# C rows spread by transposes of a broadcast column instead of one bf16 matmul, and unit 7 of each step turned like the other odd units

## The reference, cut to what matters

```python
xs = jnp.concatenate([x_hwwh, x_hwwh[..., ::-1]], axis=1)          # 4 paths, L = 128
x_dbl = jnp.einsum('bkdl,kcd->bkcl', xs, x_proj_w)                 # 8 + 16 + 16 rows
dts, Bs, Cs = jnp.split(x_dbl, [DT_RANK, DT_RANK + D_STATE], axis=2)
dts = softplus(einsum('bkrl,kdr->bkdl', dts, dt_projs_w) + dt_projs_b)
def step(h, inp):                                                  # for each of the 128 positions
    u, dt, Bl, Cl = inp
    h = h * jnp.exp(dt[..., None] * A) + (dt * u)[..., None] * Bl[:, :, None, :]
    return (h, jnp.einsum('bkdn,bkn->bkd', h, Cl))                 # D_STATE = 16 states n
```

## Time and profile before

| | |
|---|---|
| median of three runs | 29268.55 us |
| the profiled execution's own time | 29284.73 us |
| its span, first to last instruction | 29282.9 us |
| PE busy | 23746.5 us (81%) |
| DVE busy | 25685.0 us (88%) |
| ACT busy | 23805.4 us (81%) |
| POOL busy | 23349.3 us (80%) |
| mean granted TensorE clock | 0.946 |

### The profile page before, as it was taken

One profiled execution on the slowest core, in us unless ns is written; L12 is line 12 of the kernel. 1 busy time (PEld: TensorE's weight loads), 2 busy tenths in 40 slices (PEclk: granted clock), 3 DMA queues, 4 the chain that ended last, 5 costly groups with the idle time before them and its releaser, 6 DMA issues.

```text
span 29282.9 us, 495306 instructions
## 1 busy us (share of the span) xinstructions
PE 23746.5 (81%) x145198; PEld 17788.1 (61%) x145198; DVE 25685.0 (88%) x24511; ACT 23805.4 (81%) x48778; POOL 23349.3 (80%) x10372
## 2 busy tenths in 40 slices
PE   5999995888888888887888888888878888888887
PEld 1656563666666666666666666666666666666666
DVE  7555555999999999999999999999999999999999
ACT  2444444998889899888888888898888888998888
POOL 4000003999999999999999999999999999999999
PEclk6999997999999999999999999999999999999999
DMA  4000003333333333333333333333333333333333
GB/s 143 26 27 26 26 27 139 108 106 106 107 106 108 106 107 106 106 107 107 106 106 106 105 108 106 107 106 106 107 107 106 107 106 107 106 106 108 106 108 97
DMA packets 2189273, 2869.65 MB, mean 98 GB/s; under 512 B 695002, under 2 KB 964858, under 8 KB 2177786
## 3 DMA queue, kind: packets, MB, share of 16 engines
q1 hardware_dynamic: 2181978, 2803.33, 31.2%
q10 hardware_dynamic: 4608, 33.82, 0.3%
HBM read 2667.01 MB, written 169.74 MB: 97 GB/s over the span
## 4 chain that ended last, share of the span: by engine, by line
ACT 27%; PE 25%; issue 16%; DVE 11%; POOL 3%; ACTq 1%; DVEq 1%; DMA 0%; SPq 0%; POOLq 0%
DVE hst L1535 10%; PE yps L1245 8%; ACT dbT L1425 6%; ACT dAs L1403 6%; ACT dA L1403 6%; PE dbx L1230 5%; PE misc L1145 5%; PE misc L1164 2%; POOL hc L1612 2%; POOL dbu L1598 1%; DVE hc L1543 1%; ACT vab L1358 1%; PE misc L1181 1%; PE cps L1221 1%; ACT vab L1344 1%
## 5 line engine op out<-in xcount | busy, mean ns | idle before, releaser
L1598 POOL TENSOR_TENSOR dbu<-dtu,bb 128x1024 f32<-128x1024 f32 x4096 | 9686.7, 2371 | 1217.2 <-DVE hst L1535 1215.0
L1535 DVE TENSOR_TENSOR_SCAN hst<-dA,dbu 128x1024 f32<-128x1024 f32 x4096 | 9347.6, 2282 | 773.1 <-ACT dA L1403 750.2
L1612 POOL TENSOR_TENSOR hc<-hst,cc 128x1024 f32<-128x1024 f32 x4096 | 9728.0, 2375 | 5.1 <-DVE hst L1535 4.0
L1245 PE MATMUL yps<-ident,hc 128*128 128x128 f32 x65536 | 8945.1, 283 | 333.0 <-POOL hc L1612 329.7
L1245 PEld LDWEIGHTS yps<-ident,hc 128*128 128x128 f32 x65536 | 7986.0, 147 | 1823.7 <-issue 1273.3
L1535 DVE TENSOR_TENSOR_SCAN hst<-dAs,dbx 128x1024 f32<-128x1024 f32 x3584 | 8117.8, 2265 | 58.8 <-issue 57.1
L1230 PE MATMUL dbx<-ident,dbT 128*128 128x128 f32 x28672 | 4153.1, 292 | 3343.6 <-DVE hst L1535 2977.8
L1230 PEld LDWEIGHTS dbx<-ident,dbT 128*128 128x128 f32 x28672 | 3391.2, 148 | 4764.1 <-DVE hst L1535 3652.8
L1425 ACT ACTIVATE dbT<-dtuT,bT 128x256 f32<-128x256 f32 x14336 | 6126.1, 495 | 18.2
L1403 ACT ACTIVATE dA<-dtv,aneg 128x508 f32<-128x508 f32 x8192 | 5291.6, 678 | 405.6 <-DVE hst L1535 402.1
L1403 ACT ACTIVATE dAs<-dtv,aneg 128x508 f32<-128x508 f32 x7168 | 4743.5, 711 | 520.1 <-DVE hst L1535 518.1
(11 more groups left out here) (188 smaller groups left out, 28222.6 us busy)
## 6 DMA issues: line engine op xcount, KB each, us to landing
bb<-l_bscr SPq DMA_DIRECT2D x1024, 1024.0 KB, 5.7
cc<-l_bscr SPq DMA_DIRECT2D x1024, 1024.0 KB, 5.5
bx<-l_bscr SPq DMA_DIRECT2D x1024, 256.0 KB, 6.1
xg<-xgp SPq DMA_DIRECT2D x512, 85.0 KB, 2.5
xgp<-xb ACTq DMA_DIRECT2D x32, 1032.0 KB, 9.4
xt<-in_x_dram SPq DMA_DIRECT2D x128, 256.0 KB, 2.8
l_xnT<-xo SPq DMA_DIRECT2D x128, 256.0 KB, 2.0
xn<-l_xnT SPq DMA_DIRECT2D x256, 128.0 KB, 2.1
```

Source lines behind the costliest of these rows:

```text
L1245: mm = pe.matmul(yps[:, p, f * P:(f + 1) * P], hc[:, u % HB, f * 512 + p * P:f * 512 + (p + 1) * P], ident[:], is_transpose=True, start=fi ...
L1535: nc.vector.tensor_tensor_scan(hst[:, v % 4, way], decays.rearrange("p f c -> p (f c)")[:, way], inputs.rearrange("p f c -> p (f c)")[:, way],
L1598: nc.gpsimd.tensor_tensor(to, dtu[:, step % 2], row.unsqueeze(1).to_broadcast([P, 2, 512]), ALU.mult).then_inc(s_inp, 1)
L1612: nc.gpsimd.tensor_tensor(hc[:, v % HB].rearrange("p (f c) -> p f c", f=2), hst[:, v % 4].rearrange("p (f c) -> p f c", f=2), row.unsqueez ...
```

## The change

It does three things.

1. `spread_c` no longer multiplies bf16 parts. It issues four 128 x 128 float32 transposes whose stationary operand is one column of the turned copy, broadcast over 128 columns. The turned copy (bT, now bcT) keeps the 16 columns of C beside the 16 of B.
2. The splits go: two jobs and two casts a step in `JOBS`, PE and ACT, the cast after xproj, its wait for s_cb, and the tiles part, selc and nident with their loading. The weight tiles wx and wdt shrink from 104 rows to 40.
3. PLAIN_ODD becomes empty: units 7, 23, 39 and 55 are turned. Which products with C are POOL's and which DVE's stays (C_EVEN = (10,)).

```diff
     UN = 4 * NST
+    DTR = 2 * NST
-    PLAIN_ODD = (7,)
+    PLAIN_ODD = ()
...
-            JOBS[XPROJ[q] + 1] = (kind, "split", (q + 1) % 4, 1)
-            JOBS[XPROJ[q] + 2] = (kind, "split", (q + 1) % 4, 2)
...
-                def spread_c(ph, u):
+                def spread_c(u):
                     step = u // NST
-                    if u % NST == 0:
-                        pe.wait_ge(s_me, ph.misc(("own" if step else "pre", "split", step, 2)))
-                    pe.matmul(cps[:, :], selc[:, u % NST], part[:, u // NST % 2], start=True, stop=True).then_inc(s_cb, 1)
+                    for p in range(4):
+                        mm = pe.transpose(cps[:, p * P:(p + 1) * P],
+                                          bcT[:, step % 2, p, u % NST:u % NST + 1].to_broadcast([P, P]), ident[:])
+                    mm.then_inc(s_cb, 1)
...
                     elif what == "xproj":
                         n = b * 4 + j[2]
                         wait(act, s_bst, n * 16 - 16)
-                        nc.scalar.copy(xdbl[0:104, j[2] % 2], misc[0:104, :])
-                        wait(act, s_cb, n * (NCD // 4) - NCD // 4)
-                        nc.scalar.copy(part[:, j[2] % 2], misc[0:96, :]).then_inc(s_me, 1)
-                    elif what == "split":
-                        r = 64 if j[3] == 1 else 32
-                        nc.scalar.copy(part[0:r, j[2] % 2], misc[0:r, :]).then_inc(s_me, 1)
+                        nc.scalar.copy(xdbl[0:DTR + 8, j[2] % 2], misc[0:DTR + 8, :]).then_inc(s_me, 1)
...
-                        nc.scalar.copy(bT[:, step % 2], cps[:].rearrange("p (w n) -> p w n", w=4)[:, :, NST:2 * NST]).then_inc(s_ce, 1)
+                        nc.scalar.copy(bcT[:, step % 2], cps[:].rearrange("p (w n) -> p w n", w=4)[:, :, 0:DTR]).then_inc(s_ce, 1)
```

More of the change, by code:

```diff
@@ L714, in layer1 @@
         pbwd = sb("pbwd", [P, 2, P])
[L715 removed]
         wconv = sb("wconv", [P, 2, 9, P])
         wz = sb("wz", [P, 2, P])
[L718 to L719 removed]
+        wx = sb("wx", [P, 4, 2, DTR + 8])
+        wdt = sb("wdt", [DTR + 8, 4, 2, P])
         wo = sb("wo", [P, 2, P])
@@ L1163, in job @@
                         for f in range(2):
-                            mm = pe.matmul(misc[0:104, :], wx[:, KS[step], f], xs[:, KS[step] % 2, f],
+                            mm = pe.matmul(misc[0:DTR + 8, :], wx[:, KS[step], f], xs[:, KS[step] % 2, f],
                                            start=(f == 0), stop=(f == 1))
@@ L1168, in job @@
                         step, f = j[2], j[3]
-                        pe.matmul(misc[:, :], wdt[:, KS[step], f], xdbl[0:104, step % 2], start=True, stop=True).then_inc(s_mf, 1)
+                        pe.matmul(misc[:, :], wdt[:, KS[step], f], xdbl[0:DTR + 8, step % 2], start=True, stop=True).then_inc(s_mf, 1)
                     elif what == "gate":
                         pe.matmul(misc[:, :], wz[:, j[2]], xg[:, :, 1:9, 1:33], start=True, stop=True).then_inc(s_mf, 1)
-                    elif what == "split":
-                        pe.matmul(misc[0:96, :], nident[:], part[:, j[2] % 2], start=False, stop=True,
-                                  skip_group_check=True).then_inc(s_mf, 1)
                     elif what == "unpermute":
@@ L1270, in _ @@
                 pe.wait_ge(s_ce, 3)
-                spread_c(PRO, 0)
+                spread_c(0)
                 fill(1, 0)
@@ L1295, in body @@
                         if u + 2 < UN and not c_pool(u + 2):
-                            spread_c(ph, u + 2)
+                            spread_c(u + 2)
                         elif u + 2 == UN and not last:
-                            spread_c(ph, 0)
+                            spread_c(0)
                         job_of(ph, u + 1)
@@ L1685, in shape_constants @@
     pbwd = np.stack([np.ascontiguousarray(pfwd[:, o * P:(o + 1) * P].T) for o in range(2)])
-    selc = np.zeros((96, 16, P), np.float32)
-    for part in range(3):
-        for n in range(16):
-            selc[32 * part + n, n, :] = 1.0
     group = np.kron(np.eye(P // 4), np.full((4, 4), 0.25)).astype(np.float32)
-    return {"group": group, "ident": np.eye(P, dtype=np.float32), "pfwd": pfwd, "pbwd": pbwd, "selc": selc}
+    return {"group": group, "ident": np.eye(P, dtype=np.float32), "pfwd": pfwd, "pbwd": pbwd}
 def build(nc, given, out, N):
@@ L1698, in build @@
     second = {name[len("L1_conv_"):]: ap for name, ap in given.items() if name.startswith("L1_conv_")}
-    consts = {name: given[name] for name in ("ident", "group", "pfwd", "pbwd", "selc")}
+    consts = {name: given[name] for name in ("ident", "group", "pfwd", "pbwd")}
     layer0(nc, {**first, **consts, "l0_ln_w": first["ln_w"], "l0_ln_b": first["ln_b"], "x": given["x"], "x1T": x1T, "xgp": xgp}, N)
```

34 lines of the change are left out of this document (13 added, 21 removed).

## The result

The changed kernel takes 29602.6 us, median of 4 runs (29556.7 to 29638.7); the kernel before, 4 runs beside it, 29269.8. The ratio is 1.0113, with a 95% interval of 1.0096 to 1.0131: slower, by 333 us and not by the 131 us that I forecast. Inside the range; the size is off by a factor of 2.5.

The account below looks back on a forecast made before the run. DVE was taken as the frame, with 10.9 us of idle time a batch. The terms summed to +1.1 us a batch, +140 us over 128 batches, less 6: from 29268.6 to about 29400 us, range 29170 to 29640.

Parts of the forecast that it names:

- unit 22/23: PE idles 3.5 us before fill(23), the clock falls in 8 of 10 batches, DVE waits; net +0.8 us a batch.
- The splits on PE: Two matmuls and their waits for ACT go; none was in front of a waiting DVE, so worth nothing.
- The spread: Four transposes into cps take 0.60 us, next group after 0.44; cps comes 0.22 us later than with bf16.
- Rival 3: The broadcast column loads slowly: +0.54 us more per spread, +415 us in all, about 29800; chance 0.06.
- Unit 60: DVE's product of unit 60 waits for cps, so the longer spread shows there: +0.22 us a batch.
- Unit 28: DVE's product of unit 28 waits for cps, so the longer spread shows there: +0.22 us a batch.
- Scan 1 and unit 2: Near the batch's start, longer spread before the product of unit 2 in some seven of ten batches: +0.1 us.
- The chain to scan 20: From fill(13) through PE's spreads and ACT to scan 20: net +0.1 us; unit 9's clock -0.3.
- Scan 44: At unit 39 dt no longer comes behind a stop and start, worth -0.15 us a batch at scan 44.
- POOL: Four instructions of 2.377 us a batch go, 1217 us over the run; costed at nothing because POOL waits for scans.
- rival 5: POOL was the bound after all: its 1217 us come off, to about 28050 at best; chance 0.02.
- Rival 4: Transposes don't count as busy PE, so the clock stays down: +11 us a batch, 30700; chance 0.01.

Follow-up runs that it names:

- e4: The changed kernel with 16 dummy transposes of zeros on PE ahead of fill(23) once a batch; 29327.9 us, ratio 1.0016 to the kernel before.
- e9: The changed kernel with the dt matmul over 104 rows instead of 40, the new rows zero; 29392.1 us, ratio 1.0041 to the kernel before.
- e16: The kernel before with the dt matmul over the 8 rows that aren't zero instead of 104; 29380.4 us, ratio 1.0014.
- e17: The changed kernel with the dt matmul over all 128 rows, the new ones zero; 29434.3 us, ratio 1.0032 to the kernel before.
- e2: The changed kernel with unit 7 plain again, leaving the spread by transposes and the removed splits; 29469.7 us, ratio 1.0064 to the kernel before.
- e18: The changed kernel with unit 7 plain again and the dt matmul over 104 rows; 29459.0 us, ratio 1.0043 to the kernel before.
- e14: The kernel before with 16 dummy transposes of zeros on PE ahead of fill(61) only; 29148.6 us, ratio 0.9956.
- e8: The kernel before with unit 7 turned, plus 12 dummy transposes at unit 6 and 12 at unit 24; 29609.7 us, ratio 1.0110.
- e12: The changed kernel with total(u - 1) ahead of the fill at units 4, 20, 36, 52, and dummy transposes at units 20 (12) and 58 (16); 29003.1 us, ratio 0.9903.
- e3: The changed kernel with total(u - 1) moved ahead of fill(u + 3) on PE at units 4, 20, 36 and 52; 29167.6 us, ratio 0.9954.
- e1: The kernel before with unit 7 turned and nothing else; bf16 parts, splits and bf16 spread stay; 30160.6 us, ratio 1.0299.
- e6: The kernel before with dummy transposes of zeros at units 0 (14), 8 (10), 58 (16) and 62 (10); 29925.7 us, ratio 1.0218.

## Why the prediction was right in its place and wrong in its size

- **The mis-sized term is unit 22/23's**, "In all 1.2 us, 1.0 on average", net +0.8. It measured +2.66 us a batch, of +2.6 in all. The mechanism is the one I wrote: the fill at the head of the queue, 3.66 us of idleness (3.5 forecast), the clock falls (in 127 of 128 batches, 8 in 10 forecast), the spread and then the softplus come late. I priced every fall by those of the earlier trace rows, which end after 3.4 us, at 1.2 us; the 60 short ones cost 1.61, and the 65 others lasted 10.2 us and cost 3.87. Had all been short, the waits would have been about 1.6 us a batch, against 1.0 forecast; the length of the long ones adds 1.1 or so. In e4, with no fall of 10.2 us and with none at all in 59 batches, 275 us come back. e9, e16 and e17 show what the length goes with: the dt matmul behind the fall, cut from 104 rows to 40 by the change. I had read "wx and wdt shrink" and given it no price. The length of a fall was not a constant of the kernel, and I took it for one.
- **The splits on PE** I put at nothing. e2, in which they are gone and unit 7 is plain, loses 0.64%, where my terms without the fill would have given less than 0.2%; 1.35 us a batch stand at unit 22, behind falls of 6.8 us. With 104 rows (e18) the falls are of 3.4 us and 0.22 us of that wait is left, so most of it goes with the rows of dt, again the part I gave no price. The part of the change without unit 7 was under-priced too.
- **The spread** took what I said: 0.60 us a group and 0.44 to the next (12658.19 to 12658.63). Rival 3 is out: 276 ns is the mean of a transpose with a broadcast column, and 285 that of the fill's, with a full tile. Unit 60 is +0.25 for +0.22. Unit 28 lost nothing. Scan 1 and unit 2 together went down by 0.16 where I had +0.1: scan 1 no longer waits, though the clock still falls near the batch's start in nearly every batch. Its wait stands in the kernels with unit 7 plain (0.46 before, 0.39 in e2, 0.81 in e14) and is under 0.1 us in those with it turned; why is open. All that lies outside unit 22/23 adds up to about nothing, where I had +0.3; terms of both signs missed, and they cancel by luck.
- **The chain to scan 20**: scan 12 to scan 20 went from 4.62 to 4.39 us together. I had +0.1 - 0.3. The shift from scan 20 to the products before it, which I named as the sign, is there: 2.09 to 1.38.
- **Scan 44** lost 0.24 where I had a gain of 0.15. No run here asks why.
- **POOL** was worth nothing, as costed (rival 5 out). **ACT**'s exchange of casts for scales was even, and e8, which has the scales and keeps the casts, waits for ACT 3 us a batch.
- **Rival 4, the page.** The changed kernel between 12655.4 and 12658.8 us ran transposes alone:

```profile
12655.40:12658.80 3.40, 3.40 (x34) 3.38 (x32) 1.71 (x3) 3.40 (x8) 2.67 (x2) 1.00 0.31 101
```

The clock is full there. The dummies of e4 and e12, transposes all, keep it from falling: at this place it fell in 127 batches without them and in 69 with them (e4), and in 85 without and none with them where total goes first (e3, e12). The Trainium skill's page "TensorE: Matmul & The Clock Gate", Part 4, says that transposes don't count as a busy PE in the same way. Here they do; the measurement decides, and the forecast of 30700 us by that rule is out.

## What to carry to other kernels

Where one engine has spare time but another waits for it in order, don't ask how much idle time it has but how long its pieces are, and what stands behind the longest: work that you take off it may slow what is left. A short filler, or an instruction pulled ahead of the one that waits, can be worth more than the work saved: e12 is 2.0% faster than the change, and the moved instruction alone (e3) 1.6%. Before you price a clock fall by one seen elsewhere, look at what runs behind it.

## What the runs showed of the hardware

- A fall of TensorE's clock at an idle piece of 3.66 us lasted 3.4 us (60 batches) or 10.2 us (65), with PE busy nearly all the time from fill(23) on. With a dt matmul of 104 or 128 rows in place of 40 none lasted 10.2 us (e9, e17); with 8 rows in the kernel before, the falls of 6.8 us went from 9 to 236 and the time at half clock from 2051 to 3173 us (e16).
- Two float32 matmuls over 40 rows kept the next group waiting for 1.05 us at full clock, two over 104 rows for 0.86 to 0.96. Why is open.
- PE stopped for 2 to 6 us for its own code near the top of the loop, and went on 0.9 to 1.8 us after a packet of the instruction queue had landed (e1, e6). With 24 dummies a batch the stop was gone (e1 to e8: 551 us), and 50 brought one into the kernel before (e6). The DMA queues were full of a load of small packets at the time. That the code's packet waits behind them is how I read it and isn't shown: no run took the load away or moved the stop from the loop's jump back, and once started such a packet took about 1 us with other packets in flight or without (e1, medians 0.96 and 1.09).
